# A graph network kernel: source scores looked up from a stationary table, edge scores made in an earlier stage, and another split of the gathered rows

## The chip, the cores and the metric

The kernel runs on one core of one Trainium2 chip. The metric is the device time of one execution in microseconds (us); a kernel's time is the median of its runs.

## The reference

Four graph layers over N = 6250 nodes and E = 106250 edges, each followed by a residual and a layer norm. The edges are sorted by destination. The first sums 128 attributes of each node's incoming edges, the second is a GIN layer, the third two SAGE layers. The fourth, which the change is about, is an attention layer with three heads (H = 3) and 16 attributes per edge:

```python
xp = (x @ W).reshape(n, H, OUT)
a_src = jnp.einsum('nhc,hc->nh', xp, att_src)
a_dst = jnp.einsum('nhc,hc->nh', xp, att_dst)
ep = (ea2 @ W_edge).reshape(-1, H, OUT)
a_edge = jnp.einsum('ehc,hc->eh', ep, att_edge)
alpha = a_src[row2] + a_dst[col2] + a_edge
alpha = jnp.where(alpha >= 0, alpha, NEG_SLOPE * alpha)
m = jax.ops.segment_max(alpha, col2, num_segments=n)
ex = jnp.exp(alpha - m[col2])
denom = jax.ops.segment_sum(ex, col2, num_segments=n)
attn = ex / denom[col2]
msg = attn[:, :, None] * xp[row2]
agg = jax.ops.segment_sum(msg, col2, num_segments=n)
```

`row2` and `col2` are the sources and destinations of the edges with one self loop per node behind them.

## The kernel before, in words

It is written by hand, one program per engine: SP and ScalarE issue most loads and stores, GpSimd (POOL) the indirect DMAs, and every dependence is a wait on a semaphore. The order on each engine is that of its program.

In order of time:

1. **The start and the first edge sums** (0 to about 820 us). The edge list is loaded, VectorE makes from it, among much else, the low eight bits of each source index (`source_parts`, lines 1985 to 1991: one instruction of 104 x 1024 and two copies) and looks for the windows of the edge list (`near_windows`, from 1993), for which GpSimd's fetches wait (`fetch`, 913). TensorE sums the 128 edge attributes by destination and builds a dense adjacency in f16.
2. **Three dense stages** (820 to 1941 us). Each multiplies a table of node rows by the adjacency in 25 blocks of 250 nodes (NP = 25), seven slices a block, that SP loads (`load_dense`, 763; matmuls L1586). Dense 1, from 1259 to 1613 us, belongs to the first SAGE layer; its blocks take 14.15 us. VectorE's part per block is `layer2`: the mean operand, a copy of the product (L2545), and the z rows. Dense 2 follows for the second SAGE layer, and stores the node rows x3 and per node the source scores `as3_d`.
3. **Scores per edge** (2006 to 2410 us). 52 steps (NIT) of 2048 edges. ScalarE loads the low source bytes of the step to all partitions (`load_low`, L1272) and its edge attributes (`load_ea`, L1259). VectorE (`score_step`) compares the low bytes with the partition's number, twice 2048 columns (L2614), which makes a one-hot operand; TensorE (`score_rows`, L1818) multiplies it as the stationary side by a small table of the source scores (75 columns, three bf16 parts), 96 matmuls a step. VectorE then makes a mask from the high bytes (L2624), the product of attributes and edge weights (L2628), the selected scores out of PSUM (L2634), and three sums (L2638, L2642, L2646). ScalarE stores the sum of source and edge score (`store_as`, L1276). All of it is loaded back as one row of 832 edges per partition.
4. **Softmax by segment scans** (2410 to 2537 us): VectorE scans forward and backward over each partition's 832 edges; attention goes to HBM.
5. **Gathers of x3 rows.** From the end of dense 2 GpSimd gathers the source row of each edge: 208 groups (NG) of 512 edges, four indirect DMAs each (`gather_chunk`, L896), 832 in all, into a ring of four buffers. The first 140 groups (STORED) are stored by SP to HBM (`store_xe`, L808) and loaded again later by ScalarE (`load_stored`, L1316) into four other buffers; the last 68 (FRESH) are used where they land.
6. **Weighted sums** (`sums`, 1515 and 2183; from about 2545 us). For each group VectorE makes one-hot and weighted operands (L2186, L2194), TensorE multiplies them by the gathered rows, 16 matmuls (L1526), and VectorE adds the result to the node sums (L2206). After four stored groups the order is two stored, one fresh, throughout. The name `slices` on the matmul means a stored group, `rows` a fresh one.
7. **The end** (from 3105 us). The self loops' weights, fetched by GpSimd behind all gathers (`loop_weights`, L1014), are turned to diagonals by ScalarE (L1351) and multiplied on TensorE (`loops`, L1845), then the last dense product, layer norm and output, to 3258 us.

What GpSimd's gathers wait for stands in front of them:

```python
            for g in range(NG):
                i = g % RING
                if RING <= g < STORED + RING:
                    pool.wait_ge(xe_stored[i], 16 * (g // RING))
                if g >= STORED + RING:
                    pool.wait_ge(group_summed, SUMMED + place(0, 3 * (g - RING - STORED) + 2) + 1)
                if SCORES_LEAD <= g < SCORES_LEAD + PASSES:
                    pool.wait_ge(scores_begun, g - SCORES_LEAD + 1)
                for c in range(CH):
                    gather_chunk(i, c, src_i[:, CH * g + c:CH * g + c + 1], t3_d, rows_landed[i])
```

The last wait spreads the first gathers over the 104 half steps of the scores (PASSES), one group of four behind each.

Of the kernel before, what the change touches and what calls it, by code (L numbers as in the profile page):

```python
# [5 lines left out]
F32 = mybir.dt.float32  # L6
I32 = mybir.dt.int32
F16 = mybir.dt.float16
BF16 = mybir.dt.bfloat16
# [4 lines left out]
P = 128  # L14
# [28 lines left out]
def gnn_stack(nc, t, out):  # L43
# [43 lines left out]
    KT = 2  # L87
    QH = 25
    SB = RING * GE
    PASSES = 2 * NIT  # L90
    SCORES_LEAD = 10
    FRESH = 68
    STORED = NG - FRESH
    MIXED = FRESH // RING
    MIX = 3 * RING
    NC = RING * CH
    BC = NC // 2
# [6 lines left out]
    assert FRESH % RING == 0 and STORED % RING == 0 and STORED == RING + 2 * RING * MIXED and STORED >= PASSES + SCORES_LEAD  # L104
    assert N % PN == 0 and NP % 2 == 1 and FULL == NG - 1 and 0 < TAIL < HE and TAIL % CW == 0
# [5 lines left out]
    with ctx:  # L111
# [21 lines left out]
        low_d = dram("src_low", (EP,), BF16)  # L133
# [5 lines left out]
        as_d = dram("src_and_edge_score", (EP, HEADS))  # L139
# [12 lines left out]
        weighted = sb("weighted", [P, RING, CH, HEADS, W])  # L152
        idx = sb("idx", [P, CH], I32)
        ea = sb("ea", [P, RING, CH, EF])
        prod = sb("prod", [P, RING, CH, HEADS, EF])
        e_score = sb("e_score", [P, RING, CH, HEADS])
# [9 lines left out]
        onehot_l = [weighted[:, :, :, :, :].rearrange("p i c h w -> p (i c h w)")[:, n * 2 * CH * LO:(n + 1) * 2 * CH * LO  # L166
                                                                                  ].rearrange("p (c n w) -> p c n w", n=2, w=LO) for n in range(2)]
        asum = sb("asum", [P, RING, CH, HEADS])
# [4 lines left out]
        key_row = sb("key_row", [P, 2, NW], F16)  # L173
        key_w, row_w = key_row[:, 0, :], key_row[:, 1, :]
        key = key_row[:, :, :].rearrange("p k w -> p (k w)").bitcast(F32)
# [34 lines left out]
        low = slices_f[:, 0:SB].bitcast(BF16).rearrange("p (s e) -> p s e", s=2)  # L210
        lowT = slices_f[:, SB:3 * SB].bitcast(BF16).rearrange("p (s b k e) -> p s b k e", s=2, b=2, k=KT)
        tab_at = 3 * SB
        tab_f = slices_f[:, tab_at:tab_at + KT * QH * HEADS].rearrange("p (q h) -> p q h", h=HEADS)
        tab_r = slices_f[:, tab_at + 150:tab_at + 300].rearrange("p (k h i) -> p k h i", k=KT, h=HEADS)
        tab_b = slices_f[:, tab_at + 300:tab_at + 525].bitcast(BF16).rearrange("p (n k h i) -> p n k h i", n=3, k=KT, h=HEADS)
# [3 lines left out]
        pow2 = sb("pow2", [1, 2])  # L219
        ident = sb("ident", [P, P])  # L220
# [6 lines left out]
        zb, rb = (zrb[0:TN, n, :, :, :] for n in range(2))  # L227
# [25 lines left out]
        rstd = sb("rstd", [TN, 2, TP])  # L253
        norm_eps = sb("norm_eps", [P, 1])

        w01 = sb("w01", [P, 2, H0 * P])
        w02 = sb("w02", [P, H0, P])
        w11 = sb("w11", [P, H1 * P])
        w12 = sb("w12", [P, H1, P])
# [2604 lines left out]
```

## Time and profile before

| | |
|---|---|
| median of 3 runs | 3265.49 us (3263.92 to 3271.52) |
| the profiled execution's own time | 3259.58 us |
| its span, first to last instruction | 3258.0 us |
| mean granted TensorE clock | 0.816 |
| TensorE matmul busy | 2370.6 us, 73% |
| VectorE busy | 1558.9 us, 48% |
| ScalarE busy | 695.8 us, 21% |
| GpSimd busy | 1423.7 us, 44% |
| moved by DMA | 627.41 MB, mean 193 GB/s |

The span is what the trace covers; the execution's own time is 1.6 us longer, and the median of the runs 5.9 us longer than that. The shares are means over stages that differ: what a stage waits for is read from its own stretch. A granted clock of 1.0 is 2.4 GHz, 0.5 is 1.2 GHz.

### The profile page before, as it was taken

What the parts mean: (1) busy time and instruction counts of PE and PEld (TensorE: products, weight loads), DVE (VectorE), ACT (ScalarE), POOL (GpSimd) and SP (SyncE); (2) the same over time, 40 slices, a digit from 0 to 9 for tenths busy, and PEclk for the clock granted to TensorE, in tenths of its full rate; (3) what the DMA queues carried; (4) which work ended last, traced back from release to release, by engine and by line L of the source; (5) the groups of instructions that cost most, each with busy time, mean ns of one, the idle gap of its engine ahead of it and who ended that gap; (6) DMA issues with size and microseconds to landing.
All of it is one profiled execution on the core that took longest, in us unless ns stands there. A gap on an engine that the chain in (4) does not pass through costs nothing. (4 is left out here: it accounts for less than half of the span.)

```text
span 3258.0 us, 68610 instructions
## 1 busy us (share of the span) xinstructions
PE 2370.6 (73%) x21724; PEld 2084.5 (64%) x21725; DVE 1558.9 (48%) x3763; ACT 695.8 (21%) x1091; POOL 1423.7 (44%) x1498
## 2 busy tenths in 40 slices
PE   3799999899999835999879982565630104999965
PEld 2677777696888724888778872565530104999954
DVE  5677676433211372111133336888879002555567
ACT  0188887564000231000010000000000100000043
POOL 4522222123000031222223447777778777776765
PEclk9999999898999957999989996888765555555577
DMA  5589999823888527888689986899862534665611
GB/s 158 145 274 293 288 297 296 264 65 91 282 281 284 162 67 249 252 249 249 189 271 283 292 237 154 192 190 186 183 153 76 167 104 123 148 147 143 144 34 43
DMA packets 560774, 627.41 MB, mean 193 GB/s; under 512 B 265887, under 2 KB 412524, under 8 KB 560041
## 3 DMA queue, kind: packets, MB, share of 16 engines
q1 hardware_dynamic: 258425, 387.60, 39.7%
q10 hardware_dynamic: 252072, 164.25, 19.2%
q0 software_dynamic: 50208, 74.70, 9.5%
q8 instruction: 35, 0.57, 0.1%
q14 instruction: 34, 0.28, 0.0%
HBM read 484.61 MB, written 142.11 MB: 192 GB/s over the span
## 5 line engine op out<-in xcount | busy, mean ns | idle before, releaser
L896 POOL DMA_INDIRECT rows<-x_rows,src_i x832 | 850.2, 1022 | 281.3 <-issue 234.6
L1586 PE MATMUL ps<-slices,wide 128*128 128x250 f16 x7350 | 828.2, 271 | 44.9 <-DMA slices<-adjacency 44.7
L1586 PEld LDWEIGHTS ps<-slices,wide 128*128 128x128 f16 x7350 | 715.9, 98 | 132.8 <-issue 24.1
L1818 PE MATMUL ps<-slices 128*128 128x75 bf16 x4992 | 240.7, 224 | 168.1 <-DVE slices L2614 167.7
L1818 PEld LDWEIGHTS ps<-slices 128*128 128x128 bf16 x4992 | 233.8, 115 | 174.9 <-issue 174.9
L931 POOL TENSOR_TENSOR ea_one<-ea,ones 128x64 f32<-128x64 f32 x250 | 129.4, 519 | 409.5 <-DMA ea<-in_edge_attr 380.5
L1526 PE MATMUL ps<-weighted,slices 128*128 128x57 f32 x1120 | 253.4, 417 | 69.3 <-DVE weighted L2194 69.3
L1526 PEld LDWEIGHTS ps<-weighted,slices 128*128 128x128 f32 x1120 | 247.2, 333 | 69.8 <-DVE weighted L2194 69.8
L1465 PE MATMUL ps<-rows,weighted 128*32 128x128 f32 x2000 | 273.0, 281 | 12.4 <-DMA ea<-in_edge_attr 9.4
L1526 PE MATMUL ps<-weighted,rows 128*128 128x57 f32 x544 | 130.6, 419 | 193.5 <-DMA rows<-x_rows,src_i 169.4
L1526 PEld LDWEIGHTS ps<-weighted,rows 128*128 128x128 f32 x544 | 123.4, 332 | 196.3 <-issue 169.5
L1465 PEld LDWEIGHTS ps<-rows,weighted 128*32 128x32 f32 x2000 | 203.0, 112 | 60.9 <-issue 53.2
L1115 ACT ACTIVATE wide<-ps 128x980 f16<-128x980 f32 (+1 forms) x182 | 195.3, 1173 | 54.2 <-PE ps L1456 29.9
L2206 DVE TENSOR_TENSOR wide<-wide,ps 128x57 f32 x416 | 89.2, 214 | 237.0 <-PE ps L1526 206.5
L1115 ACT ACTIVATE slices<-ps 128x980 f16<-128x980 f32 (+1 forms) x168 | 180.4, 1176 | 39.1 <-DMA adjacency<-slices 25.2
L1351 ACT ACTIVATE hT<-ident,wloop 125x125 f32<-125x125 f32 x150 | 46.0, 386 | 605.2 <-PE ps L1526 544.6
L954 POOL MEMSET wide<- 128x6250 f32 x3 | 15.9, 5311 | 352.7 <-PE ps L1695 349.7
L2339 DVE SCALAR_TENSOR_TENSOR wide<-ps,scale,wide 128x250 f32 (+1 forms) x75 | 35.8, 478 | 254.7 <-PE ps L1586 251.5
L1456 PE MATMUL ps<-aT,prod 128*128 128x245 f16 x650 | 102.5, 276 | 32.6 <-ACT slices L1115 16.1
L2545 DVE COPY yb<-ps 125x256 f32<-125x256 f32 x25 | 10.6, 424 | 239.2 <-PE ps L1738 239.2
L2194 DVE TENSOR_TENSOR weighted<-onehot,att 128x228 f32<-128x228 f32 x208 | 82.7, 397 | 70.7 <-DMA att<-attention 70.7
L1468 PEld LDWEIGHTS ps<-ea_one,weighted 128*32 128x32 f32 x2000 | 102.7, 114 | 20.3 <-POOL ea_one L931 19.6
(356 smaller groups left out, 3429.5 us busy)
## 6 DMA issues: line engine op xcount, KB each, us to landing
slices<-adjacency SPq DMA_DIRECT2D x525, 437.5 KB, 5.4
rows<-in_edge_attr SPq DMA_DIRECT2D x250, 256.0 KB
adjacency<-wide ACTq DMA_DIRECT2D x91, 437.5 KB, 4.2
adjacency<-slices ACTq DMA_DIRECT2D x84, 437.5 KB, 3.7
x_of_edges<-rows SPq DMA_DIRECT2D x140, 256.0 KB
slices<-x_of_edges ACTq DMA_DIRECT2D x140, 256.0 KB
slices<-src_low ACTq DMA_DIRECT2D x52, 512.0 KB
rows<-x_rows,src_i POOLq DMA_INDIRECT x832
```

Of the source, the lines that this page charges most:

```text
L896: pool.indirect_dma_start(out=packed[i][:, c, :], out_offset=None, in_=table, in_offset=bass.IndirectOffsetOnAxis(ap=rows_of, axis=0)).the ...
L931: pool.tensor_tensor(ea_one[:, i, :, 1:NSUM], ea[:, i, :, :], ones[:, 0:CH * EF].rearrange("p (c f) -> p c f", f=EF), ALU.mult).then_inc(e ...
L1115: act.activation(to[:, x:x + size, :, :], ps_k[n % 2][:, 0:size, :].rearrange("p x (q r) -> p x q r", r=WN), ACT.Copy).then_inc(key_copied, 1)
L1351: op = act.activation(diag[:, s, k, h, :], ident[0:TN, 0:TN], ACT.Copy, scale=wloop_f[:, bass.ds(HEADS * (TP * q + k) + h, 1)])
L1456: mm = pe.matmul(ps_k[n % 2][:, x, :], row_1h[j % 2][:, g, :, i], key_1h[j % 2][:, g, :, i], start=True, stop=True)
L1465: pe.matmul(to[:, 0:P], onehot_l[i // 2][:, c, i % 2, :], packed[i][:, c, :], start=(c == 0), stop=(c == CH - 1))
L1468: mm = pe.matmul(to[:, P:P + NSUM], onehot_l[i // 2][:, c, i % 2, :], ea_one[:, i, c, :], start=(c == 0), stop=(c == CH - 1))
L1526: mm = pe.matmul(ps_a[i][:, width * h:width * (h + 1)], of[:, n, :], weighted[:, i, n, :, :].rearrange("p h w -> p (h w)"), start=(c == 0) ...
L1586: mm = pe.matmul(ps_d[b], high_low[:, part, QS * s + q, :], slices[:, s, PN * q:PN * (q + 1)], start=(s == 0 and q == 0 and part == 0), st ...
L1818: mm = pe.matmul(ps_g[:, s, b, c, 0:HEADS * QH], lowT[:, s, b, h, P * c:P * (c + 1)], tab_b[:, n, h, :, :].rearrange("p h i -> p (h i)"), ...
L2194: v.tensor_tensor(weighted[:, i, :, :, :], onehot[:, i, :, :].unsqueeze(2).to_broadcast([P, CH, HEADS, W]), att[:, i, :, :].unsqueeze(3).t ...
L2206: v.tensor_tensor(acc, acc, part, ALU.add).then_inc(psum_free, 1)
```

## The change

- **The source score lookup.** Three key parts (KT = 3, of 128 nodes each) and 17 high values (QH) in place of 2 and 25. The table, scaled by a power of two and split into two f16 parts (102 columns, QR), is the stationary side; the one-hot of the low parts is the moving side, 512 columns a matmul. The low parts are loaded as one row and spread over the partitions by a matmul with a row of ones and two ScalarE copies (`spread_low`, `copy_low`). The high parts are loaded as bytes to 102 partitions; one VectorE instruction per half step compares them and takes the selected scores out of PSUM (`picked`); a second small matmul sums them (`sum_picks`). The scores are stored by head.
- **The edge scores** leave the score steps. SP loads the attributes in dense 1, 32 edges (512 floats) of 127 partitions with each block (`load_ea`), and VectorE multiplies and sums them in `layer2` (`edge_scores`). The last partition, which is not full, comes by a pass of its own (`ea_end`, `es_end`, `es_d`). The result stays in SBUF until the softmax adds it.
- **The split.** STORED goes from 140 to 108 groups, FRESH from 68 to 100; after eight stored groups, stored and fresh alternate. The gathers' wait on `scores_begun` goes.
- **Beside these:** `source_parts` is seven instructions instead of three, the scale of the scores is worked out ahead of dense 1's work (`score_scale`), some waits of the scans are split, and several buffers share memory.

The diff, cut to its core:

```diff
-    KT = 2
-    QH = 25
+    KT = 3
+    QH = 17
...
-    FRESH = 68
+    MIXED = NP
+    FRESH = RING * MIXED
     STORED = NG - FRESH
-    MIXED = FRESH // RING
-    MIX = 3 * RING
+    FIRST = 2 * RING
+    MIX = 2 * RING
+    ESC = 32
...
         def is_fresh(j):
-            return j % 3 == 2
+            return j % 2 == 1
...
+            def load_ea(c, i):
+
+                to = rows[0:P - 1, 1 + i, :, :].rearrange("p c f -> p (c f)")[:, 0:ESC * EF]
+                sp.dma_start(to, ea16[0:(P - 1) * EPP, :].rearrange("(p j) e -> p (j e)", j=EPP)[:, bass.ds(ESC * EF * c, ESC * EF)]
+                             ).then_inc(es_in[i], 16)
...
                 def body(q, u, b, first):
                     for s in range(SL):
+                        if k == 1 and s == SL - 2:
+                            if not first:
+                                sp.wait_ge(es_made, 2 * q - 1)
+                            load_ea(q, b)
...
-                if SCORES_LEAD <= g < SCORES_LEAD + PASSES:
-                    pool.wait_ge(scores_begun, g - SCORES_LEAD + 1)
...
+            def next_scores(k, s, first=False, begun=False, last=False):
+
+                u = 2 * k + s
+                copy_low(u + 2, s, 0)
+                if first and s == 1:
+                    store_as(0, 0, True)
+                elif not first:
+                    store_as(k - 1 + s, 1 - s, first=begun)
+                copy_low(u + 2, s, 1)
+                if not last:
+                    load_low(u + 4, s)
+                act.wait_ge(picked_ready, 2 * u + 2)
+                load_hi(u + 2, s)
...
+            def score_pass(k, s, first=False, last=False):
+
+                u = 2 * k + s
+                score_rows(u, s, 0, first)
+                if not (first and s == 0):
+                    sum_picks(u - 1, 1 - s, 1, first)
+                if not last:
+                    spread_low(k + 1, s, 0)
+                score_rows(u, s, 1, first)
+                sum_picks(u, s, 0, first)
+                if not last:
+                    spread_low(k + 1, s, 1)
...
+            def edge_scores(c, u, i):
+
+                ea_c = rows[0:P - 1, 1 + i, :, :].rearrange("p c f -> p (c f)")[:, 0:ESC * EF].rearrange("p (j e) -> p j e", e=EF)
+                v.wait_ge(es_in[i], 16 * (u + 1) + (16 if i == 0 else 0))
+                if isinstance(c, int) and c == 0:
+                    v.tensor_reduce(es_end[:, :, :], products(0, ea_end, EST, P), AX.X, ALU.add).then_inc(es_made, 1)
+                v.wait_ge(es_made, 2 * c + 2)
+                v.tensor_reduce(es[0:P - 1, :, bass.ds(ESC * c, ESC)], products(c + 1, ea_c, ESC, P - 1), AX.X, ALU.add).then_inc(es_made, 1)
...
-            def lows(n, s):
-
-                v.wait_ge(low_in[s], n)
+            def lows(u, s):
+
+                v.wait_ge(low_copied, 2 * u + 2)
                 for k in range(KT):
-                    op = v.tensor_scalar(lowT[:, s, :, k, :], low[:, s, :].rearrange("p (b e) -> p b e", b=2),
-                                         slot_p[:, k:k + 1], None, ALU.is_equal)
+                    op = v.tensor_scalar(lowT[:, s, k, :], low[:, s, :], slot_p[:, k:k + 1], None, ALU.is_equal)
                 op.then_inc(lowT_ready, 1)
...
+                v.wait_ge(hi_in[s], 16 * (k + 1))
                 for b in range(2):
                     v.wait_ge(g_summed, 2 * u + b + 1)
...
+                    if not (first and s == 0):
+                        v.wait_ge(picks_summed, 2 * u + b - 1)
+                    v.scalar_tensor_tensor(picked[:, b, :], hi_b[:, s, SH * b:SH * (b + 1)], seg_i[0:QR, 0:1], ps_g[:, b, :],
+                                           ALU.is_equal, ALU.mult).then_inc(picked_ready, 1)
```

## Rows read from the trace of the kernel before

**Rows 1.** One line's instructions: count, ns min/median/max, first to last start.

```profile
L896 POOL DMA_INDIRECT rows<-x_rows,src_i x832: 938/944/5533, 1961.6 to 3086.6; - x167
```

**Rows 2.** Line 896 by stretch: stretch, us, POOL busy (count), PEclk, DMA share, GB/s.

```profile
2006.00:2410.00 404.00, 309.45 (x310) 0.81 0.88 185
2410.00:2537.00 127.00, 104.75 (x74) 0.50 0.36 109
2537.00:2726.00 189.00, 142.77 (x152) 0.50 0.41 118
2726.00:3090.00 364.00, 257.72 (x269) 0.50 0.60 145
```

**Rows 3.** Groups of instructions, 2537 to 2726 and 2726 to 3090 us.

```profile
L896 POOL DMA_INDIRECT rows<-x_rows,src_i x152 | 143.5, 944 | 46.3 <-issue 46.3
...
L896 POOL DMA_INDIRECT rows<-x_rows,src_i x269 | 257.7, 958 | 104.0 <-issue 67.9 <-PE ps L1526 36.1
```

**Rows 4.** Timeline, 2722 to 2760 us: start, length, engine, [idle before, releaser].

```profile
2731.02 1.95 PE L1526 MATMUL ps<-weighted,rows 128*128 128x57 f32 x8 [169.36 <-DMA rows<-x_rows,src_i]
...
2732.77 3.62 PE L1526 MATMUL ps<-weighted,slices 128*128 128x57 f32 x16
```

**Rows 5.** Busy time by stretch: us, PE, PEld, DVE, ACT, POOL, PEclk, DMA, GB/s.

```profile
2006.00:2410.00 404.00, 240.68 (x4992) 233.80 (x4992) 351.37 (x575) 0.00 (x0) 309.45 (x310) 0.81 0.88 185
1290.00:1560.00 270.00, 270.00 (x2212) 240.04 (x2211) 31.42 (x76) 25.60 (x59) 57.30 (x57) 1.00 0.83 249
```

**Rows 6.** Groups of instructions, 2006 to 2410 us.

```profile
L2634 DVE TENSOR_TENSOR hT<-ps,hT 128x600 f32<-128x600 f32 x104 | 76.2, 772 | 2.8 <-PE ps L1818 2.8
L2614 DVE TENSOR_SCALAR slices<-slices,slot_p 128x2048 bf16<-128x2048 bf16 x104 | 76.0, 772 | 22.0 <-DMA slices<-src_low 19.0 <-issue 2.6
...
L2628 DVE TENSOR_TENSOR prod<-ea,we_b 128x768 f32<-128x768 f32 x52 | 50.0, 961 | 23.1 <-DMA ea<-in_edge_attr 20.4 <-issue 2.1
```

**Rows 7.** Groups of instructions, 1290 to 1560 us.

```profile
L1586 PE MATMUL ps<-slices,wide 128*128 128x250 f16 x1866 | 209.8, 269 | 0.0
```

**Rows 8.** The page, costliest groups of instructions.

```profile
L1115 ACT ACTIVATE wide<-ps 128x980 f16<-128x980 f32 (+1 forms) x182 | 195.3, 1173 | 54.2 <-PE ps L1456 29.9
```

**Rows 9.** Timeline, 2024 to 2027 us.

```profile
2024.90 1.05 POOL L896 DMA_INDIRECT rows<-x_rows,src_i  x1 [0.31 <-issue]
2025.07 1.42 DVE L2614 TENSOR_SCALAR slices<-slices,slot_p 128x2048 bf16<-128x2048 bf16 x2 [1.13 <-DMA slices<-src_low]
2025.10 0.36 ACTq L1272 DMA_DIRECT2D slices<-src_low  x1
...
2026.25 1.06 POOL L896 DMA_INDIRECT rows<-x_rows,src_i  x1 [0.30 <-issue]
```

**Rows 10.** Timeline, 2492.5 to 2495 us.

```profile
2492.87 2.76 DVE L2747 TENSOR_TENSOR wide<-wide 128x2496 f32<-128x2496 f32 x1
...
2493.89 2.54 POOL L896 DMA_INDIRECT rows<-x_rows,src_i  x1 [0.30 <-issue]
```

**Rows 11.** Timeline of VectorE, 1562 to 1580 us.

```profile
1566.15 0.42 DVE L2545 COPY yb<-ps 125x256 f32<-125x256 f32 x1 [9.77 <-PE ps L1738]
```

**Rows 12.** Timeline, 60 to 100 us.

```profile
69.97 0.69 DVE L1987 TENSOR_SCALAR wide<-wide 104x1024 int32<-104x1024 int32 x1
...
78.64 1.75 POOL L915 DMA_INDIRECT slices<-dst_filled,at_w  x1 [3.26 <-DVE at_w L2003]
...
86.52 1.23 DVE L2023 SCALAR_TENSOR_TENSOR slices<-wide,slices 104x1024 f32<-104x1024 f32 x1
```

**Rows 13.** Timeline, 3078 to 3150 us.

```profile
3087.85 1.31 POOL L1014 DMA_INDIRECT wloop<-loop_weight,end_i  x1 [0.30 <-issue]
...
3105.58 4.64 PE L1845 MATMUL ps<-hT,xb 125*128 125x375 f32 x8 [1.57 <-DVE wide L2206]
...
3111.81 1.84 ACT L1351 ACTIVATE hT<-ident,wloop 125x125 f32<-125x125 f32 x6 [10.59 <-DMA wloop<-loop_weight,end_i]
```

**Rows 14.** Line 1014, the loop-weight fetches: issue to landing.

```profile
DMA to landing us min/median/max: 2.5/3.4/4.1
```

More of the change, by code:

```diff
@@ new lines, in _ @@
+            for s in range(2):
+                next_scores(0, s, first=True)
+            next_scores(1, 0, begun=True)
+            next_scores(1, 1)
+            with act.Fori(2, NIT // 2 - 2) as k:
+                for s in range(2):
+                    next_scores(k, s)
+            for s in range(2):
+                next_scores(NIT // 2 - 2, s, last=True)
+            store_as(NIT // 2 - 2, 1)
+            for s in range(2):
+                store_as(NIT // 2 - 1, s)
+            for s in range(2):
+                act.wait_ge(as_stored[s], 16 * HEADS * (NIT // 2))
@@ L1715, in _ @@
             pe.wait_ge(prep_dve, NODE_DVE + 3)
+            pe.wait_ge(prep_dve, NODE_DVE + 4)
+            pe.matmul(ps_m[:, 320:321], ones[:, :], bound[:, 0:1], start=True, stop=True).then_inc(prep_pe, 1)
             missing_groups(missing2_i)
@@ L1827, in _ @@
+            for s in range(2):
+                for b in range(2):
+                    spread_low(0, s, b, first=True)
             pe.wait_ge(prep_dve, MAX_DVE + 3)
-            with pe.Fori(0, NIT // 2) as k:
+            for s in range(2):
+                score_pass(0, s, first=True)
+            with pe.Fori(1, NIT // 2 - 1) as k:
                 for s in range(2):
-                    for b in range(2):
-                        score_rows(k, s, b)
+                    score_pass(k, s)
+            for s in range(2):
+                score_pass(NIT // 2 - 1, s, last=True)
@@ L2233, in mixed @@
                         if not (last and j + 2 >= MIX):
-                            weights(p + 2, 1 + 3 * u + (j + 2) // RING, (j + 2) % RING)
-                        add(p, j % RING, fresh[j // 3] if is_fresh(j) else stored[stored_at(j)])
+                            weights(p + 2, 2 + 2 * u + (j + 2) // RING, (j + 2) % RING)
+                        add(p, j % RING, (fresh if is_fresh(j) else stored)[j // 2])
                 with v.Fori(0, MIXED - 1) as u:
@@ L2373, in layer0 @@
                 layer_norm(d0, s, n + 1, rb, yb, d0.done)
[L2375 removed]
+            part = [sums_b[:, n * HEADS * P:(n + 1) * HEADS * P] for n in range(2)]
             def weights_beside(q, s):
```

404 lines of the change are left out of this document (227 added, 177 removed).

## The prediction

> **What bounds the kernel now.** I asked first when GpSimd's gathers of x3 rows run. The 832 of them start between 1961.6 us and 3086.6 us, so the series ends at 3087.5 [rows 1], and the busy time by stretch shows GpSimd at work in every part of it [rows 2]. The groups of instructions say what an undisturbed gather costs: 152 of them fill the 189 us from 2537 us, 1.243 us each, 0.944 of work and 0.30 of issue [rows 2, 3]. Then TensorE in order of time: it sits idle for 169 us until the first fresh group lands at 2731 us, and from there it is full, 16 matmuls in 3.62 us, 1.81 us a group [rows 4]. In that last stretch GpSimd in its turn waited 36.1 us for summed groups [rows 3]. So the score stretch (2006 to 2410 us), in which VectorE is busy for 351 of 404 us [rows 5], does not set the end: TensorE could have begun to sum 169 us before it did. What sets the end is the gather series, up to 2731 us alone, from there in turn with TensorE.
>
> 832 gathers at 1.243 would be 1034 us; the series took 1126, so 91.8 us are excess. By stretch: score 404 - 310 x 1.243 = 18.7; scans 127 - 74 x 1.243 = 35.0; last 361.6 (2726 to the series' end) - 269 x 1.243 = 27.2; the first 45 us hold the other 10.9 [rows 2]. Of the 27.2: the 67.9 of plain issue gaps are 222 gathers at the 0.305 of the undisturbed ones (46.3 over 152), so the other 47 waited for TensorE, and beyond an issue gap that is 36.1 - 47 x 0.30 = 22.0, longer gathers 269 x (0.958 - 0.944) = 3.8; 1.4 is left [rows 3].
>
> **Fewer stored groups.** Stored groups go from 140 to 108, fresh ones from 68 to 100, and after eight groups the two kinds alternate. Eight groups are 14.5 us of TensorE (8 x 1.81) and hold four fresh ones, 16 gathers, 19.9 us of GpSimd. TensorE now waits for GpSimd and not the reverse: the 22.0 us go. The first fresh group is gathers 433 to 436 in place of 561 to 564, so it lands some 150 us earlier; what is late next is the gather series itself. The gathers' own wait on score passes goes too: it lies in the 18.7, at most 7 by what is left over below, and I give it nothing.
>
> **The score lookup.** A step is 2048 edges, 52 steps. VectorE gets three comparisons of 2048 columns at 0.772 and two selections of 1024 columns out of PSUM, by the 600-column one at 0.772 no more than 1.32 each: 4.9 us where it is 6.8 (351 over 52) [rows 5, 6]. TensorE: 12 table matmuls, 4 sums, 4 spreads, all of 512 columns; the dense products take 0.112 us for 250 columns at the full clock (209.8 us over 1866) [rows 7], so 0.23 each, 4.6 us. ScalarE: two evictions of 1024 columns (980 take 1.17) [rows 8], one of 12 rows by 512 (0.4 to 0.8; I take 0.6), five DMA issues at 0.36 [rows 9]: 4.8 us. The three are tied. The second spread waits for the eviction of the first (one PSUM buffer); behind that eviction in ScalarE's order stand three score stores; VectorE's comparisons of a later step wait for the second eviction. Selection, sum, spread and eviction in series after the comparisons give about 6 us a step, 52 x 6 = 312 us, 92 less than now. On the path this is worth nothing: the score stretch's end, with scans and first groups behind it, comes before gather 449, the first that must wait for a summed group. That cover holds up to a step of 8.7 us (rival A).
>
> **What comparisons do to gathers.** The gathers beside a pair of comparisons take 1.05 and 1.06 [rows 9], undisturbed ones 0.944: 0.22 a step, 11.4 us in all. The other 7 of the 18.7 lie beside two-operand products (edge products, slot selection), which go. 156 comparisons in place of 104 give 17. The selections read PSUM like the present ones; I add nothing. Bounds: 0, and 156 x 0.772 = 120 if each holds GpSimd throughout; I take 17, by the nearest rows. The softmax gains one full-width two-operand instruction like the one of 2.76 us, beside which a gather took 2.54, so 1.6 more [rows 10]; otherwise it lies inside the wait for the scores' reload. The Trainium skill (SBUF — State Buffer, "Who interferes with whom") says that VectorE in a two-port mode takes the shared port pair for its whole instruction and GpSimd blocks fully. Read to the letter this speaks against three comparisons in a row and gives the upper bound. [...]
>
> So the series' excess becomes 10.9 + 17 + (35.0 + 1.6) + (27.2 - 22.0) = 69.7: **22.1 us shorter**.
>
> **Edge scores in the second dense stage.** VectorE gains a product and a sum of 1536 columns per block; by twice the 768-column product (0.961) for each, at most 3.9 us [rows 6]. They stand behind the mean operand, in a gap of 9.77 us in which VectorE waits for TensorE [rows 11]. Their added wait for loaded edge rows stands ahead of the z copy, on which TensorE's next second layer depends; but the rows were asked for one block, 14 us, earlier. The one call behind the loop runs while z is stored and the next table loads. Loads: 127 x 2 KB per block, 26 of them, 6.8 MB. The stage moves 249 GB/s at 0.83 of the DMA engines, and TensorE is busy for 270 of 270 us [rows 5]: the load makes 7% more, 0.89. Cost nothing; if that cover is not there, 6.8 MB at 249 GB/s are 27 us. On SP's queue each is one issue (0.36) ahead of two slice loads, and waits for an edge product two blocks back. The load of the last partition's attributes stands ahead of the first slice load, for which TensorE waits: +0.4. Of SP's new waits ahead of the x-row stores, all are for things done well before. The score scale is some twelve tiny instructions and a matmul inside the wait for the table load.
>
> **Source parts at the start.** Seven instructions of 1024 columns in place of one and two halves: six of 0.69 and one of 1.23, 5.4, less 1.4 now: 4.0. They stand on VectorE ahead of the window search, for which GpSimd's queue already waits 3.26 us [rows 12], and twenty fetches hang behind that. Nothing covers them: +4.0; bounds 0 and 5.4. The new constants and the removed memset lie under the first loads.
>
> **The end.** GpSimd is through with gathers at 3087.5, and the first loop matmul starts at 3105.6, 18 later; the loop weights were fetched meanwhile [rows 13]. When gathers are last, two loop-weight fetches follow them (1.6 each), landing (3.4) [rows 14] and six diagonal copies (1.84) [rows 13]: 8.4, say 9, with the last sum (about 7) beside it. **-9**; bounds -5 and -12. The 154 us behind stay.
>
> **Sum**: -22.1 + 0.4 + 4.0 - 9 = -26.7 against the profiled execution's 3259.6: 3232.9. The median of the runs shown, 3265.5, is 5.9 above that execution; against it, 3238.8. About 0.3%, 9.8 us, is what a measurement can tell here.
>
> **Rivals.**
> A, slower: the matmuls run at the lower clock. The score stretch is granted 0.81, and the tail from 2410 us on 0.50 although TensorE is full there [rows 2, 4]. At 1.2 GHz 20 matmuls take 9.2 us and the stretch ends at 2006 + 478 = 2484. Gather 449 waits for the tenth group: six were summed at 2561.7 (2731.0 - 169.4) [rows 4] and four more take 7.2, so 159 after the score stretch; 384 gathers follow at 1.262: the series ends at 3128, 40 later than now, and with +4.4 and -9 it is +35: 3301. It decides from 8.7 us a step. Against it: 75-column matmuls got 0.81, 250-column ones 1.00 [rows 2, 5]. Chance 0.07.
> B, slower: comparisons in threes hold GpSimd for half their length, 156 x 0.386 = 60 in place of 17: +16, 3282. The rows show a third of it; this is half of what the skill's port rule would give. 0.06.
> C, no change: the attribute loads are not hidden in a stage at 0.83: +27, 3266. 0.10.
> D, more gained: no excess from comparisons, start hidden, the end at -12: 17 + 4.4 + 3 more, 3214. 0.08.
> E, the 92 us of the score stretch reach the end, with -9 and +4.4: 3169. The gather series speaks flatly against it. 0.03.
> The lookup may not be faster at all; up to 8.7 us a step that changes nothing and is inside the forecast.
>
> **Chances.** Forecast 0.62, its own range 3226 to 3253; 0.04 for the same mechanism with terms that come to under 9.8. Faster: 0.62 + 0.08 + 0.03 = 0.73. Same: 0.10 + 0.04 = 0.14. Slower: 0.07 + 0.06 = 0.13. The range from 3214 to 3272 leaves out A, B and E, 0.16.
>
> **What would show it.** Right: a gather series some 22 us shorter, with no wait on TensorE; TensorE waiting for gathered rows throughout the last stretch; score steps of about 6 us; dense blocks of 14 us as now; the start 4 us later; 9 us from the last gather to the first loop matmul. Wrong: gathers that wait somewhere else, or a series of more than 1.33 us per gather; then the sum falls, whatever the score stretch does.

## The result, and the profile after

The changed kernel takes 3400.84 us (median of 4 runs, 3398.89 to 3402.86) against 3264.7 for the kernel before: 1.041 times as long, interval 1.0394 to 1.0426. The forecast was 3238.8 with a range up to 3272, so it is wrong in sign and far out of its range. The profiled execution has a span of 3401.1 us, 143.1 more than before.

I split the 143.1 us at four points, each read from the starts of one line's instructions: the first dense matmul (L1644, before L1586), the last second-layer matmul of dense 1 (L1799, before L1738), and the first and last gather (L938, before L896). First for the kernel before, then for the changed one (count, ns min/median/max, first to last start, shape):

```profile
L1586 PE MATMUL ps<-slices,wide x7350: 267/269/415, 820.8 to 1940.6; 128*128 128x250 f16 x199
...
L1738 PE MATMUL ps<-w,hT x200: 379/379/481, 1280.9 to 1616.9; 128*125 128x256 f32 x100
```

```profile
L1644 PE MATMUL ps<-slices,wide x7350: 267/269/415, 825.7 to 2110.5; 128*128 128x250 f16 x199
...
L1799 PE MATMUL ps<-w,hT x200: 379/379/481, 1294.8 to 1786.0; 128*125 128x256 f32 x100
...
L938 POOL DMA_INDIRECT rows<-x_rows,src_i x832: 940/945/5284, 2128.3 to 3242.2; - x167
```

| stretch | before | after | difference |
|---|---|---|---|
| start, to the first dense matmul | 820.8 | 825.7 | +4.9 |
| to the last second-layer matmul of dense 1 | 796.1 | 960.3 | **+164.2** |
| to the first gather | 344.7 | 342.3 | -2.4 |
| gather series, to the end of the last | 1125.9 | 1114.8 | -11.1 |
| behind it | 170.5 | 158.0 | -12.5 |

The tail answers to [rows 13]: the first two fetches of loop weights behind the gathers, the diagonals made from them, and the first loop matmul, 6.7 us after the last gather's end.

```profile
3243.48 1.29 POOL L1056 DMA_INDIRECT wloop<-loop_weight,end_i  x1 [0.31 <-issue]
...
3245.07 1.27 POOL L1056 DMA_INDIRECT wloop<-loop_weight,end_i  x1 [0.30 <-issue]
...
3247.80 1.85 ACT L1410 ACTIVATE hT<-ident,wloop 125x125 f32<-125x125 f32 x6 [643.51 <-DMA wloop<-loop_weight,end_i]
...
3249.94 4.79 PE L1945 MATMUL ps<-hT,xb 125*128 125x375 f32 x8 [1.56 <-ACT hT L1410]
```

The start and the tail are near what the prediction has, and the series falls short of it. The line that decides is dense 1. Of its 164.2 us, 155 lie in the 24 distances between its second-layer matmuls (14.0 us each before, 20.5 after) and 9 ahead of the first of them. The busy time of its stretch (us, PE, PEld, DVE, ACT, POOL, PEclk, DMA share, GB/s; the row of before is in [rows 5]):

```profile
1290.00:1560.00 270.00, 213.36 (x1540) 177.52 (x1540) 67.05 (x79) 17.70 (x41) 39.12 (x39) 0.90 0.57 184
```

TensorE is no longer full, 213 of 270 us, and yet the DMA engines are *less* busy than before, 0.57 in place of 0.83, and move 184 GB/s in place of 249. So the stage waits for data while the DMA engines, taken together, are idle 43% of the time. The waits of dense 1 in the changed kernel name the data (total us, times, longest):

```profile
PE ps L1644 <- DMA slices<-adjacency: 104.8, 24, 6.0
```

These waits are 4.4 us of the 6.5 that a block is longer. The rest is in the main TensorE's own time, about 16 us a block in place of 14.0: it was granted 0.90 in this stretch in place of 1.00 (in the rows below it stands at 0.50 at 1405 us, behind a wait of 5.1 us that ended at 1403.7, and at 1.00 at 1407), and the mean dense matmul took 291 ns instead of 269.

The DMA issues of 1320 to 1600 us say how late they are (the last number is the median from issue to landing), in the changed kernel and then in the kernel before:

```profile
slices<-adjacency SPq DMA_DIRECT2D x92, 437.5 KB, 9.4
rows<-in_edge_attr SPq DMA_DIRECT2D x13, 254.0 KB
```

```profile
slices<-adjacency SPq DMA_DIRECT2D x138, 437.5 KB, 4.3
```

The busy time cut into single microseconds shows why. Ahead of it the issue of one load of edge attributes in the timeline of SP's queue; then the stretches behind it (us, PE busy, PEclk, DMA share, GB/s):

```profile
1402.62 0.26 SPq L780 DMA_DIRECT2D rows<-in_edge_attr  x1
```

```profile
1405.00:1406.00 1.00, 1.00 (x7) 0.50 0.94 369
1406.00:1407.00 1.00, 1.00 (x7) 0.50 0.82 329
1407.00:1408.00 1.00, 1.00 (x11) 1.00 0.12 46
...
1412.00:1413.00 1.00, 1.00 (x7) 1.00 0.08 28
1413.00:1414.00 1.00, 1.00 (x10) 1.00 0.07 25
1414.00:1415.00 1.00, 1.00 (x11) 1.00 0.76 130
1415.00:1416.00 1.00, 1.00 (x12) 1.00 0.94 366
```

The share falls from 0.9 to 0.12, rises to 0.47 while the slice issued at 1406.9 comes in, and then stands at 0.08 and 0.07, about one sixteenth, with 25 to 28 GB/s: **that is what one DMA engine of sixteen makes**. Behind it the share is back at 0.76 and more. The next two blocks show the same (0.07 at 1441 us, 0.08 and 0.06 at 1453 and 1454). The load is a DMA of 127 partitions. The profile gives a mean over the sixteen engines and not which of them is busy, so this is a reading, and the experiments have to test it.

The Trainium skill states this rule ("DMA: Bandwidth & Descriptors", section "Why a DMA increments its semaphore by 16 and not by 1"): a DMA runs on as many engines as the largest number up to 16 that divides the slowest dimension (other than 1) of both its access patterns, which makes one engine for 127 partitions. The prediction did not draw on it. The runs below order the blocks as this rule would for 127, 122 and 112 partitions (20.5, 15.7 and 14.0 us); none of them counts the engines themselves.

### The profile page after: what moved, and what is told of

Same layout as the page of the kernel before. It is cut to its first block, busy times and chain, and to the rows that moved or that the text cites. A ratio compares the mean times of both kernels' runs of the same rounds, so it can differ in the third digit from the quotient of the medians.

```text
span 3401.1 us, 60425 instructions
## 1 busy us (share of the span) xinstructions
PE 2464.9 (72%) x17774; PEld 1968.4 (58%) x17775; DVE 1537.0 (45%) x3512; ACT 825.7 (24%) x1247; POOL 1433.7 (42%) x1502
## 3 DMA queue, kind: packets, MB, share of 16 engines
q10 hardware_dynamic: 132995, 132.97, 12.3%
## 4 chain that ended last, share of the span: by engine, by line
PE 31%; POOL 25%; DMA 24%; issue 11%; ACT 4%; DVE 3%; SPq 1%; ACTq 1%; DVEq 0%; POOLq 0%
POOL rows L938 24%; PE ps L1644 16%; DMA slices<-adjacency 15%; PE ps L1524 3%; PE ps L1515 2%; ACT wide L1155 2%; ACT slices L1155 2%; DMA x_rows<-yb 1%; DMA adjacency<-wide 1%; PE ps L1585 1%; PE ps L1710 1%; PE ps L1711 1%; PE ps L1681 1%; DMA adjacency<-slices 1%; DMA wloop<-loop_weight,end_i 1%
## 5 line engine op out<-in xcount | busy, mean ns | idle before, releaser
L1644 PE MATMUL ps<-slices,wide 128*128 128x250 f16 x7350 | 866.2, 278 | 156.2 <-DMA slices<-adjacency 156.0
L938 POOL DMA_INDIRECT rows<-x_rows,src_i x832 | 861.7, 1036 | 255.8 <-issue 249.5
L1644 PEld LDWEIGHTS ps<-slices,wide 128*128 128x128 f16 x7350 | 733.3, 100 | 266.4 <-DMA slices<-adjacency 123.2
L1585 PE MATMUL ps<-sums_b,rows 128*128 128x57 f32 x800 | 195.2, 423 | 265.1 <-DMA rows<-x_rows,src_i 198.4
L1585 PEld LDWEIGHTS ps<-sums_b,rows 128*128 128x128 f32 x800 | 178.2, 328 | 282.1 <-issue 168.9
L1524 PE MATMUL ps<-rows,sums_b 128*32 128x128 f32 x2000 | 277.8, 284 | 14.7 <-DMA ea<-in_edge_attr 10.3
L1585 PE MATMUL ps<-sums_b,slices 128*128 128x57 f32 x864 | 205.3, 417 | 70.6 <-DVE sums_b L2302 70.4
L1524 PEld LDWEIGHTS ps<-rows,sums_b 128*32 128x32 f32 x2000 | 205.6, 113 | 64.6 <-issue 54.0
L1585 PEld LDWEIGHTS ps<-sums_b,slices 128*128 128x128 f32 x864 | 196.4, 333 | 71.0 <-DVE sums_b L2302 70.7
L1879 PE MATMUL ps<-slices 128*102 128x512 f16 x624 | 158.4, 391 | 7.6 <-DVE slices L2756 7.6
L1310 ACT ACTIVATE wide<-ps 128x1024 f16<-128x1024 f32 x104 | 106.5, 1024 | 208.8 <-PE ps L1901 198.1
L2756 DVE TENSOR_SCALAR slices<-wide,slot_p 128x2048 f16<-128x2048 f16 x156 | 108.7, 753 | 54.6 <-ACT wide L1310 54.5
L2769 DVE SCALAR_TENSOR_TENSOR aT<-hT,seg_i,ps 102x1024 f16<-102x1024 uint8 x104 | 127.8, 1266 | 5.0 <-PE ps L1879 5.0
```

Source lines behind the costliest of these rows:

```text
L938: pool.indirect_dma_start(out=packed[i][:, c, :], out_offset=None, in_=table, in_offset=bass.IndirectOffsetOnAxis(ap=rows_of, axis=0)).the ...
L1310: act.activation(low[:, s, SH * b:SH * (b + 1)], ps_s, ACT.Copy).then_inc(low_copied, 1)
L1524: pe.matmul(to[:, 0:P], onehot_l[i // 2][:, c, i % 2, :], packed[i][:, c, :], start=(c == 0), stop=(c == CH - 1))
L1585: mm = pe.matmul(ps_a[i][:, width * h:width * (h + 1)], of[:, n, :], weighted[:, i, n, :, :].rearrange("p h w -> p (h w)"), start=(c == 0) ...
L1644: mm = pe.matmul(ps_d[b], high_low[:, part, QS * s + q, :], slices[:, s, PN * q:PN * (q + 1)], start=(s == 0 and q == 0 and part == 0), st ...
L1879: mm = pe.matmul(ps_g[:, b, SQ * c:SQ * (c + 1)], tab_b[:, h, :, :, :].rearrange("p n h i -> p (n h i)"), lowT[:, s, h, SH * b + SQ * c:SH ...
```

## The experiments

Series below is the time from the first gather's start to the last one's end; block is the distance from the first to the last second-layer matmul of dense 1, divided by 24 (14.0 us before, 20.5 after). Edits 1 to 5 are made on the changed kernel, each alone; edits 6 to 10 on the version of edit 1, which is called the version; the last on the kernel before.

**1. The load in two parts, 112 and 15 partitions.**

```diff
-                sp.dma_start(to, ea16[0:(P - 1) * EPP, :].rearrange("(p j) e -> p (j e)", j=EPP)[:, bass.ds(ESC * EF * c, ESC * EF)]
-                             ).then_inc(es_in[i], 16)
+                of = ea16[0:(P - 1) * EPP, :].rearrange("(p j) e -> p (j e)", j=EPP)[:, bass.ds(ESC * EF * c, ESC * EF)]
+                sp.dma_start(to[0:112, :], of[0:112, :]).then_inc(es_in[i], 16)
+                sp.dma_start(to[112:P - 1, :], of[112:P - 1, :]).then_inc(es_in[i], 16)
...
-                v.wait_ge(es_in[i], 16 * (u + 1) + (16 if i == 0 else 0))
+                v.wait_ge(es_in[i], 32 * (u + 1) + (16 if i == 0 else 0))
```

> The changed kernel with one edit: each block's load of edge attributes in dense 1, 127 partitions of 2 KB in one DMA, is issued as two DMAs of 112 and 15 partitions; same bytes, same place in SP's queue. In the changed kernel dense 1 takes 164 us more than before, some 6.6 us a block. Theory S (shape: the 127 packets of one load run one behind another on a single DMA engine, which then has about 12 us of them and 7 to 8 us of slices to move in every block of 14): the blocks come back to about 14.2 us and the time to 3235 to 3250. Theory O (order or bytes: the load stands ahead of two slice loads in SP's queue, or its 6.8 MB are simply too much): the same bytes at the same place, so 3395 to 3405. Theory V (VectorE's products and sums ahead of the z copy hold TensorE): 3395 to 3405.

Measured: 3234.1 us, 0.990 of the kernel before (0.9868 to 0.9934). The block is 14.0 us and the stage's row is again that of a full TensorE, with the DMA engines a little busier than before; under it the second-layer matmuls' line:

```profile
1290.00:1560.00 270.00, 270.00 (x2216) 240.19 (x2214) 96.43 (x114) 25.36 (x58) 57.69 (x58) 1.00 0.87 267
```

```profile
L1800 PE MATMUL ps<-w,hT x200: 378/379/482, 1286.3 to 1622.3; 128*125 128x256 f32 x100
```

The same bytes at the same place in the queue, in another shape: theory S. All 164 us are gone (795.6 us for the stretch that took 796.1 before and 960.3 in the changed kernel).

**2. Without the loads.** The 26 calls of `load_ea` and the wait for them taken out; the edge scores are then made from whatever lies in the buffers.

> The changed kernel without the 26 loads of edge attributes in dense 1 (the product and the sum work on whatever stands in the buffers, so the edge scores of the first 127 partitions are left out in effect); VectorE's instructions stay. Theory S and theory O: dense 1 is back to blocks of 14.2 us, 3235 to 3250. Theory V: 3395 to 3405. Beside the split load it shows what the loads still cost once they are spread: the difference of the two, 0 to 5 us if they are hidden.

Measured: 3227.8 us (one run); the block is 14.0 us, as with the split load. So the loads, once spread, cost dense 1 nothing; the 6 us between the two runs lie in the first stage (818.8 against 826.7 to the first dense matmul), which varied by such amounts between kernels that are alike there.

**3. Products and sums for one edge in 32.** The other edge scores are left out.

```diff
-                v.tensor_reduce(es[0:P - 1, :, bass.ds(ESC * c, ESC)], products(c + 1, ea_c, ESC, P - 1), AX.X, ALU.add).then_inc(es_made, 1)
+                v.tensor_reduce(es[0:P - 1, :, bass.ds(ESC * c, 1)], products(c + 1, ea_c[:, 0:1, :], 1, P - 1), AX.X, ALU.add).then_inc(es_made, 1)
```

> The changed kernel with the loads as they are, but product and sum made for one edge in 32 (the other edge scores are left out). VectorE has 3.4 us less per block ahead of the z copy. Theories S and O: 3395 to 3405, the blocks stay at 20.7 us. Theory V: 14.2 us blocks, 3235 to 3300.

Measured: 3402.1 us (one run), block 20.5. VectorE's work in dense 1 has no part in it: theory V falls.

**4. The loads on ScalarE's queue.** `load_ea(q + 1)` issued at the end of ScalarE's `hidden2`, none by SP.

> The changed kernel with the same loads of 127 partitions in one DMA each, issued by ScalarE on its own queue, one block ahead, and none on SP's. It tells the two readings of the load apart. If one DMA engine is too full (theory S), it stays so whichever queue hands the packets over: 3385 to 3405, blocks of 20 us. If it is the place in SP's queue ahead of two slice loads (theory O), the slices flow past: 3235 to 3260.

Measured: 3384.7 us (one run), block 19.8. Taking the load out of SP's order gave back 18 of the stage's 164 us and left 146, so the order is about a tenth of it, and theory O falls.

**5. The load in parts of 122 and 5 partitions.** As edit 1 with 122 for 112.

> The changed kernel with each attribute load cut at 122 and 5 partitions. If a load runs on as many DMA engines as is the largest divisor of its partitions up to 16, 122 partitions run on two (61 packets each, 5.5 to 6 us) and 5 on five. With 7.7 us of slices that is 13 to 14 us per block on the fullest engine, just under the block of 14.15: theory S gives blocks of 14.1 to 15 us and a time of 3230 to 3260. If instead 127 alone is the odd case and 122 spreads over all engines, 3230 to 3240 as with 112 and 15; if every load that is no multiple of 16 runs on one engine, 3385 to 3400.

Measured: 3289.1 us (one run) where the kernel before took 3277.7 on the same chip, block 15.7 us: `L1800 ... 1291.3 to 1668.6`. It issues two DMAs a block, as run 1 does, so two in place of one is not what helped there; the cut is. Theory S was right about the case between, but I had its size too low: 15.7 is over the 14.1 to 15 I gave, and 3289.1 over the 3230 to 3260. I had counted 7.7 us of slices on each engine, where the queues' rows give 11.6 us of all traffic. An estimate from these rows comes near all of the blocks. In dense 1 of the kernel before, over 280 us:

```profile
q1 hardware_dynamic: 24814, 64.56, 76.2%
q0 software_dynamic: 4930, 5.01, 6.4%
```

That is 82.6% of 14.0 us, 11.6 us per block on each engine if they share it evenly. The attributes of a block, 254 KB at 25 GB/s an engine (the lower figure of the rows above), are 10.4 us for one engine, 5.2 for two, 0.65 for sixteen:

| partitions of the load | engines by the rule | fullest engine, us per block, estimated | block measured |
|---|---|---|---|
| none | | 11.6 | 14.0 |
| 112 + 15 | 16, 15 | about 12.3 | 14.0 |
| 122 + 5 | 2, 5 | about 17 | 15.7 |
| 127 | 1 | 22 | 20.5 |

Where the estimate is below TensorE's 14.0 the load is hidden; where it is above, the block follows it, 1 to 1.5 us under. The even share and the rate are assumptions, and no view gives the load of a single engine.

With the cause shown, the other runs ask what the rest of the change is worth.

**6. The old split of the groups (140 stored, 68 fresh) in that version.**

```diff
-    FRESH = RING * MIXED
+    FRESH = 68
...
-    MIX = 2 * RING
+    MIX = 3 * RING
...
-            return j % 2 == 1
+            return j % 3 == 2
```

> The version with the split load (112 + 15 partitions, 3234.1 us) with the stored and fresh groups as in the kernel before: 140 stored, 68 fresh, two stored to one fresh; lookup and edge scores stay as changed. Theory G (the gather series and its turns with TensorE set the end, the score stretch does not): the 22 us of gathers waiting for TensorE come back and so do the 9 to 12 us at the end, some 33 us in all: 3262 to 3272, a series of about 1135 us. Rival L (the gain is the lookup's, whose stretch is 110 us shorter): 3230 to 3240, the split is worth nothing.

Measured: 3278.1 us beside 3277.7 for the kernel before, ratio 1.0001 (0.9989 to 1.0013). The series is 1136.5 us, and the wait for TensorE is back near the figure of [rows 3], 34.8 us for 36.1; from the last gather to the first loop matmul it is 18 us again:

```profile
L943 POOL DMA_INDIRECT rows<-x_rows,src_i x269 | 258.3, 960 | 102.7 <-issue 67.9 <-PE ps L1591 34.8
```

Everything of the change but the split, a score stretch some 100 us shorter with it (the table matmuls span 291.7 us in place of 393.3), comes out level with the kernel before: the lookup's gain does not reach the end. What the later start and the comparisons' hold on the gathers cost stands in the same sum and is not separated by this run. In the same run TensorE waits 291.7 us for its first fresh group where it waited 169.4 before [rows 4]: that is where the lookup's gain went.

**7. Slower score steps.** Each ScalarE copy of the low parts made twice.

```diff
+                act.activation(low[:, s, SH * b:SH * (b + 1)], ps_s, ACT.Copy).then_inc(tab_zero, 1)
+                act.wait_ge(tab_zero, 2 * u + b + 2)
                 act.activation(low[:, s, SH * b:SH * (b + 1)], ps_s, ACT.Copy).then_inc(low_copied, 1)
```

> The version with the split load, with each ScalarE copy of the low parts made twice, in series, so that a score step takes 7.7 us in place of 5.6 and the score stretch some 110 us more. VectorE and GpSimd have the same instructions. Theory G: gather 449 is the first that waits for a summed group, and the work behind the scores starts 150 us before the first fresh group lands; 110 us more fit in, so 3229 to 3240 and a gather series of 1112 to 1116 us. Rival L: the end moves by the 110 us, 3340; anything between says that the cover is shorter than I read it.

Measured: 3244.0 us, 0.9897 of the kernel before (0.9880 to 0.9913), where the version has 0.9901. The table matmuls span 350.5 us in place of 289.9, so the stretch grew by 61 us and not by 110 (that part of the second copies lies beside other work is my guess, not read from a row), and the series is 1110.8 us. 61 us more in the scores cost nothing; the full 110 were not reached.

**8. Two comparisons instead of three** (and 8 of the 12 table matmuls; the scores of a third of the source nodes are left out).

> The version with the split load, with two of the three comparisons of a score step and 8 of its 12 table matmuls: the third key part is left out, so the scores of a third of the source nodes are missing. In the version a gather beside the three comparisons takes 1.42 us against 0.94. Theory M (every comparison holds GpSimd by its share): 0.16 us a step less, 8 us over 52 steps, a gather series of about 1105 us in place of 1113.7. Rival N (the hold does not depend on how many follow each other, as the 1.05 and 1.06 beside two in the kernel before): 0.27 us a step less and more, a series of 1098 to 1102. No effect would be 1112 to 1116. The time itself moves by no more than 15 us.

Measured: 3220.0 us (one run), series 1092.4: 21 us shorter, more than either theory gave. It did a second thing. The score stretch of the version, then of this kernel:

```profile
2010.00:2302.00 292.00, 265.73 (x1032) 92.18 (x1032) 230.68 (x258) 126.31 (x151) 227.39 (x213) 0.98 0.47 136
```

```profile
2014.00:2402.00 388.00, 386.71 (x824) 91.13 (x824) 201.48 (x208) 126.31 (x151) 294.44 (x308) 0.51 0.48 134
```

With a third of its table matmuls gone TensorE was granted 0.51, the lower of its two levels (1.2 GHz), and the stretch became 96 us *longer*. The time did not grow with it, which is a second run for the score stretch's cover. A third comparison is gone too and the steps are longer, so the 21 us can't be put down to the number of comparisons alone.

**9 and 10. The three comparisons set apart** by the selections: two, selection, one, selection; and one, selection, one, selection, one. The edit of the first, at its core:

```diff
-                if not (last and s == 1):
-                    lows(u + 1, 1 - s)
+                ahead = not (last and s == 1)
+                if ahead:
+                    v.wait_ge(low_copied, 2 * u + 4)
+                    lows_of((0, 1), 1 - s)
...
                     v.scalar_tensor_tensor(picked[:, b, :], hi_b[:, s, SH * b:SH * (b + 1)], seg_i[0:QR, 0:1], ps_g[:, b, :],
                                            ALU.is_equal, ALU.mult).then_inc(picked_ready, 1)
+                    if ahead and ((2,), ())[b]:
+                        lows_of(((2,), ())[b], 1 - s)
```

> The version with the split load, complete, with VectorE's order in a score step changed: two comparisons of the next step, first selection, third comparison, second selection. The kernel with two comparisons had a gather series of 1092.4 us, 21 shorter than with three, more than a share per comparison would give; a gather beside two took at most 1.04 us, beside three 1.42. Theory R (a gather is held by comparisons that follow each other without a gap, and three in a row reach over its whole length): the pair and the single one hold it as little, 1.0 to 1.05 us each, so the series is 1095 to 1103 us and the time 11 to 18 us under the version's. Theory M (held by the sum of the comparisons, wherever they stand): series 1112 to 1116, no change.

> The same with all three comparisons apart: one, first selection, one, second selection, one. Theory R: no gather beside more than a single comparison and a step somewhat longer, which the cover of the score stretch takes (60 us more cost nothing): a series of 1090 to 1100 us, the same as or a little under that with two and one. Theory M: 1112 to 1116.

> The version with the split load once more, on the chip of the two reordered ones, as the yardstick for them: about 0.990 of the kernel before, a gather series of 1112 to 1115 us.

Measured on one chip: 3292.4 us (1.0043, 1.0023 to 1.0062) with two and one, 3338.8 us (1.0187, 1.0159 to 1.0214) one by one, 3250.2 us (0.9918, 0.9888 to 0.9948) for the version; series of 1162, 1207 and 1115 us. Both theories fall: the series grows where one had it shorter and the other unchanged. With two and one the table matmuls span 272.3 us, 17 less than in the version, and the kernel is 42 us slower all the same: the time goes with the series and not with the score stretch. The timeline of the version first, then that of two and one:

```profile
2204.32 2.08 DVE L2757 TENSOR_SCALAR slices<-wide,slot_p 128x2048 f16<-128x2048 f16 x3 [1.09 <-ACT wide L1311]
2204.47 1.42 POOL L939 DMA_INDIRECT rows<-x_rows,src_i  x1 [0.30 <-issue]
...
2206.19 1.02 POOL L939 DMA_INDIRECT rows<-x_rows,src_i  x1 [0.30 <-issue]
2206.33 2.46 DVE L2770 SCALAR_TENSOR_TENSOR aT<-hT,seg_i,ps 102x1024 f16<-102x1024 uint8 x2
```

```profile
2204.53 1.27 DVE L2779 SCALAR_TENSOR_TENSOR aT<-hT,seg_i,ps 102x1024 f16<-102x1024 uint8 x1
2205.07 2.22 POOL L939 DMA_INDIRECT rows<-x_rows,src_i  x1 [0.30 <-issue]
...
2205.72 0.75 DVE L2763 TENSOR_SCALAR slices<-wide,slot_p 128x2048 f16<-128x2048 f16 x1
...
2206.39 1.27 DVE L2779 SCALAR_TENSOR_TENSOR aT<-hT,seg_i,ps 102x1024 f16<-102x1024 uint8 x1
```

A gather takes 1.42 us beside three comparisons and 2.22 us where one comparison stands between two selections with no gap. Over the 220 us from 2050 us the median gather takes 0.99 us in the version, 1.12 with two and one and 1.94 one by one. The instructions are the same in all three, so how long a gather is held depends on their order and not only on their sum. What rule gives 1.42 and 2.22 is left open.

**11. The new split alone, in the kernel before** (the diff of edit 6 reversed; old lookup, gathers' wait on the score passes kept).

> The kernel before with the new split of the groups alone (108 stored, 100 fresh, alternating after eight; the old lookup, the edge products in the score steps, the gathers' wait on score passes). With the old split the version was level with the kernel before (1.000), with the new one 0.990. Theory G (the split is all that pays): no gather waits for TensorE, so a series of 1100 to 1108 us, 6 to 7 us from the last gather to the first loop matmul, 0.987 to 0.991 of the kernel before. Rival K (the new split needs the shorter score stretch, since the sums now begin 110 us later and gather 449 must wait for the tenth summed group): gathers wait for TensorE again, a series of 1115 to 1130 us and 0.993 to 1.000.

Measured: 3572.4 us beside 3452.6 for the kernel before on that chip, 1.0339 (1.0323 to 1.0355). The chip differed from the others. With the old lookup the table matmuls spanned 667 us here, against 387 in the run below; TensorE's matmuls stood for 319 us with nothing in the profile that they waited for. Gather 449, the first that must wait for a sum in this split (it is gather 577 in the kernel before), then did so; first the line's totals, then its own row:

```profile
L893 POOL DMA_INDIRECT rows<-x_rows,src_i x832: 938/944/1542, 1966.0 to 3404.9; - x167
...
  remote: 189.1, 89
  PE ps L1522: 174.0, 5
```

```profile
2838.87 0.94 POOL L893 DMA_INDIRECT rows<-x_rows,src_i  x1 [166.09 <-PE ps L1522]
```

So the cover is real and has an end: this one wait is 166 us. The 189.1 us in 89 waits that the profile calls remote stand in none of the other traces; what they are, and why the stretch was so long on this chip, is not shown. The question was put again on another chip, with the version beside it.

> The kernel before with the new split alone, once more. On a chip where the kernel before takes 3260 to 3280 us and its score stretch 404 us: the tenth summed group is done at about 2563 us and gather 449 is due at 2580, a margin of 17 us. Theory G (margin holds): a series of 1100 to 1108 us and 0.987 to 0.991 of the kernel before. Rival K (it doesn't): GpSimd waits for the sums at gather 449, a series over 1115, 0.993 or more. On a chip where the score stretch is much longer: again over 1.02.

> The version with the split load on the same chip. At the usual length of the score stretch 0.990 of the kernel before, level with e13 by theory G, 10 us or more ahead of it by rival K. Should the chip be one where the old score stretch takes 667 us, the shorter lookup decides: gather 449 does not wait, and the version is far ahead of both, 0.95 or less of the kernel before.

Measured: 3231.6 us, 0.9897 (0.9876 to 0.9918), for the split alone, and 3237.0 us, 0.9917 (0.9899 to 0.9936), for the version; the kernel before took 3263.4. The series is 1106.2 us with the old lookup and 1114.3 with the new one:

```profile
L893 POOL DMA_INDIRECT rows<-x_rows,src_i x832: 940/945/5553, 1966.0 to 3071.3; - x167
...
  PE ps L1522: 9.1, 30
```

30 waits of 9.1 us in all are no more than 30 issue gaps. The two times can't be told apart. A constant and the order of the groups, in the kernel before, give all that pays in this change, on a chip where the score stretch is of the usual length.

## Why the prediction was wrong

- **The step that failed** is the one on the loads of edge attributes: "Loads: 127 x 2 KB per block, 26 of them, 6.8 MB ... the load makes 7% more, 0.89. Cost nothing; if that cover is not there, 6.8 MB at 249 GB/s are 27 us." Both halves divide the bytes by the rate of all DMA engines together. The load behaved as one engine's work: by the estimate above that engine had 11.6 us per block already and got 10 more, the blocks went from 14.0 to 20.5 us, and the price was 164 us. Runs 1, 4 and 5 show it (14.0 us in two parts of 112 and 15, 19.8 from another queue, 15.7 at 122 and 5). The prediction's own sign, dense blocks of 14 us, is the one that failed. Rival C had the right place and the sign, and its size was wrong by the same step, so that no case of the forecast reached the result.
- **What bounds the kernel**: right. The score stretch came down from 404 to 294 us (312 forecast), a step from 7.8 to 5.6 us (6 forecast), and the end did not move by it: run 6 shows it level with the kernel before, runs 7 and 8 show 61 and 96 us more of it without effect. The cover's end, 8.7 us a step in the prediction, comes out lower from its own rows: the tenth group would be summed at 2568.9 (2561.7 + 7.2) and gather 449 starts at 2582.5 in the trace of before, a margin of 13.6 us over 404, so about 8.0 a step. No run lay between 7.8 and 12.8. A group is 8 matmuls in 1.81 us, as the prediction has it, and not the 16 of the description of the kernel.
- **The split**: right. The 22.0 us of gathers that waited for TensorE went. TensorE waits for rows instead: 198.4 us in 53 waits of the changed kernel, of which the first is 129.7 (the 169.4 of before in one) and the other 52 are 68.7. Behind the series -12.5 where -9 was taken, the bound being -12: the first loop matmul starts 6.7 us after the last gather (18 before). The sum of 8.4 counts the second fetch twice: its landing is timed from its start, 3245.07, and the diagonals start 2.7 us later, so its own 1.6 is inside the landing.
- **The series**: -11.1 and, without the fault, -12.3, where -22.1 was forecast. The term too small is the comparisons': the score stretch of the version (from 2007 to 2301, 214 gathers) is 294 - 214 x 1.243 = 28 us over quiet gathers, where 17 was taken and rival B had 60; the 1.05 and 2.54 us of [rows 9] and [rows 10] were a pair and a product of two operands, neither of them three comparisons in a row. "By the nearest rows" took 0.11 a comparison from a pair, and a third one behind the pair made the hold of one gather a step 0.48 (1.42 less 0.944). Scans (36.7, forecast 36.6) and last stretch (about 4, forecast 5.2) came as worked out.
- **The edge scores on VectorE** in the dense stage: nothing, as forecast (run 3, and a full TensorE in run 1).
- **Rival A**, the lower clock: the version was granted 0.98 in the score stretch, and run 8, at 0.51, had steps of 7.5 us, not the 9.2 that would have decided.
- **The start**: +4.9 where +4.0 was taken; on one chip 826.3 against 822.2 for the old start (the two runs of the last experiment), but kernels with the same start lay between 818.8 and 836.5, so the agreement shows little.
- **The sum**: with the load in two parts, the version is 28.5, 27.1 and 26.4 us under the kernel before on three chips, where -26.7 was worked out (3234.1 on the first, against a forecast of 3238.8). That closeness is part luck. Between the two traces, of different chips, the spans differ by 22.4: the series gave 9.8 us less than forecast, the end 3.5 more, and 3.0 came ahead of the first gather, where the prediction had nothing.

## What to carry to other kernels

Price a DMA by the engines that it runs on, not by its bytes alone: look at its outermost count before its size, and cut a count like 127 into one that divides well and a small rest (here 112 and 15, which took 164 us off). In this stage, at 0.83 of the DMA engines, one full engine set the pace, and the sign was a DMA share that fell (0.57) beside a stage that grew. And before a stretch is made shorter, ask which wait ends behind it: here a lookup made 110 us faster gave nothing, and a change of the order in which groups are summed gave 1%.

## What had not been expected of the hardware

- With the DMA share at one sixteenth, 25 to 28 GB/s were moved. A DMA of 127 x 2 KB then holds one engine for some 10 us (an estimate: 254 KB at 25 GB/s), and the price stood whichever queue issued it (20.5 us blocks from SP's, 19.8 from ScalarE's).
- A gather beside two comparisons of 2048 columns took 1.04 us at most (run 8), beside three 1.42; beside a comparison between two selections it took 2.22, where quiet ones take 0.94.
- TensorE, with 4 of a step's 20 matmuls taken out (and VectorE with one comparison less), was granted 0.51 instead of 0.98, and the table matmuls of 512 columns took 637 ns on average in place of 393. Which of the two brought it is not separated.
- The old lookup's table matmuls spanned 667 us on one chip and 387 and 393 in the two other traces that hold them; the kernel before took 3452.6 us there and 3262.6 to 3277.7 on the others.
